# Two graph layers on one core: wider squares and a fifth difference buffer in the statistics pass, whole-megabyte loads and a shorter softmax tail in the score pass

## The chip, the cores and the metric

One core of a Trainium2 chip runs the whole program. The metric is the device time of one execution in microseconds (us); lower is better. Three runs of the kernel before are given, and one more execution was taken by the hardware profiler.

## The reference

The input x has 32 batches of 256 rows of 128 channels. A first graph attention layer and a layer norm give the x of the second layer, which is where the time goes and where the change lies. Cut to its core:

```python
D = jnp.abs(x[:, :, None, :] - x[:, None, :, :])          # every pair of rows of a batch
h = jnp.einsum('bijc,oc->bijo', D, W1) + b1                # 128 channels -> 64
m = jnp.mean(h, axis=(0, 1, 2)); v = jnp.mean((h - m) ** 2, axis=(0, 1, 2))
h = _leaky((h - m) / jnp.sqrt(v + EPS) * g1 + be1)
s = jnp.einsum('bijo,uo->biju', h, W2)[..., 0] + b2[0]
A = jax.nn.softmax(jnp.where(A_init > 0, s, NEG), axis=-1)
y = jnp.einsum('bij,bjc->bic', A, x)
y = y @ Wg.T + bg
y = _leaky((y - mean(y)) / sqrt(var(y) + EPS) * gg + beg)  # moments over batches and rows
out = jnp.concatenate([x, y], axis=2) @ Wt.T + bt          # then x + out, layer norm
```

The moments of h go over all pairs of all batches, so the pairs are passed over twice: once for the sums (the statistics pass), once for the scores (the score pass).

## The kernel before, in words

Channels lie on the 128 partitions. `ring` holds every batch transposed, each half followed by its own beginning, so that "row j minus row i" for many pairs is one subtraction of two windows of `ring`. By symmetry only half of the pairs are computed: 16 chunks of 2048 pairs for each batch. A chunk goes through TensorE with `w1t` (`project`, L872 to L877: four matmuls of 512 columns, two to each half of the partitions), and 128x1024 values of h come out in PSUM.

**Statistics pass.** The chunks of a batch are taken in the order `ORDER`. Five of them (`ON_PE`, positions 0, 3, 6, 9 and 12 of the order) get their differences from TensorE (`pick_differences`, L879) and their absolute value from ScalarE (L610, L612), the other eleven from VectorE: `subtract` (L1217) and then `absolute` (L1233, a bitwise AND), in groups of 2, 2, 2, 2 and 3 (`differences_between`). The differences stand in a ring of `ND` = 4 buffers `diff`: `subtract` of chunk c waits until chunk c - 4 has been projected. h goes to one of two PSUM buffers `hps`; TensorE may project chunk c (`stat_chunk`, L895) once ScalarE has read chunk c - 2. ScalarE's reader is `sum_h` (L614). Four chunks (`REDONE`: positions 0, 3, 6, 9) are squared straight from PSUM with a sum (L632) and thrown away. The other twelve are copied with a sum to one of eight buffers `tokeep` (L622), which SyncE stores to DRAM (`keep`, L386: `kept_one` holds the second halves of the four thrown-away ones' rectangles, 512 KB each, `kept_two` the rest), and after every second copy the two neighbouring copies are squared side by side, 2048 wide, with a sum (L627). The square waits on the copy just before it and writes to `spare`, a part of `yt` that nobody reads.

ScalarE's own order there is the program's: for each position j of a batch `sum_h(b, j)`, and behind it `absolute(b, j + 3)` where j + 3 is one of TensorE's.

**Score pass.** A batch is eight steps `kk`. At the even steps one thrown-away chunk is made again: VectorE's `differences` and `absolutes` (L1351, L1356, two buffers), TensorE's `again` (L936), and ScalarE's leaky activation out of PSUM into `fresh` (L654, 1024 wide). Beside it stands what was kept, loaded from DRAM by SyncE (`load_kept`, L404): at even steps one of four buffers `kept1` (1024 wide), at odd steps one of three buffers `kept2` (2048 wide). Each is activated in place (L654), and `score_products` (L943, four matmuls of 512 columns) adds the step to the batch's scores in PSUM. A load waits until the step that last used its buffer has been multiplied.

In between, spread over the next batches' steps, runs the softmax of the scores: `take_scores` (L670) copies them out, SyncE stores them (four DMAs) and reads them back as blocks (seven DMAs, L432), GpSimd masks (L511), VectorE adds masks (`add_upper` L1363, `masked` L1374), ScalarE takes exponentials (L682), TensorE transposes them (`transpose_probs`), ScalarE copies (L688), TensorE multiplies with x (`aggregate`), VectorE divides by the sum (`normalise_agg`, L1387), TensorE transposes back, ScalarE copies (`aggt_out`, L692), TensorE multiplies with Wg (`second_projection`), ScalarE adds bg and writes `yt` (`y_out`, L696), VectorE takes its moments and adds bt to the rows (`y_statistics`, L1396). The step at which each engine does each of these is written out by hand in a loop over `g` at the end of each engine's program, and every engine works strictly in that order. After the last batch the loops run on for 28 steps (`LAST`).

The last stage normalises y, multiplies with Wt, adds and normalises the rows and stores them.

## Time and profile before

| | us |
|---|---|
| median of 3 runs | 2411.68 (2410.97 to 2411.91) |
| the profiled execution | 2408.98, of which the trace spans 2406.7 |
| first layer, layer norm, ring | 0 to 373 of the span |
| statistics pass | 373 to 1678 |
| score pass | 1678 to 2358 |
| last stage | 2358 to 2407 |
| busy over the span | TensorE 84%, VectorE 88%, ScalarE 91% |
| granted TensorE clock, mean | 0.980 |

The stage bounds are the starts of the first `subtract` (372.7), of the first `differences` (1678.0) and of the last `y_statistics` (2358.0). The busy shares are means over stages that differ; what a stage costs is read below as a period, the time from one batch to the next, since both passes repeat exactly from batch to batch.

### The profile page before, as it was taken

The page shows a single profiled execution, that of the slowest core. Times are in us where ns is not written, and L with a number is a line of the kernel's source. Part 1 is how long each engine was busy: PE and PEld are TensorE (multiplying, and loading weights), DVE is VectorE, ACT ScalarE, POOL GpSimd, SP SyncE. Part 2 cuts the span into 40 slices and gives each one's busy share as a digit, 9 for nine tenths or more (in the row PEclk, how much of TensorE's full clock was granted, in tenths as well). Part 3 has the DMA queues.
Part 4 walks back from the last instruction along what each step waited for, and adds up shares of the span by engine and source line. Part 5 has one row for each costly group of instructions (what it writes and reads, how often), then busy time and mean ns, then how long its engine had stood idle before and what let it go on. Part 6 is the DMA issues. An engine that isn't in the chain of part 4 may idle for free.

```text
span 2406.7 us, 35438 instructions
## 1 busy us (share of the span) xinstructions
PE 2015.1 (84%) x12869; PEld 798.3 (33%) x12869; DVE 2112.7 (88%) x2615; ACT 2196.0 (91%) x3084; POOL 47.8 (2%) x50
## 2 busy tenths in 40 slices
PE   5777767888888888888888888887898988888986
PEld 4555543323232323232323232322122222222225
DVE  5888868999999999999999999998888888888866
ACT  5999977999999999999999999996999999999985
POOL 0000000000000000000000000000000001000000
PEclk8999989999999999999999999998999999999997
DMA  4111105444444444444444444444899899999962
GB/s 117 41 40 43 45 15 173 180 169 179 169 179 169 180 168 180 169 180 168 180 169 180 169 180 169 180 168 160 335 352 348 330 346 341 339 337 333 336 238 71
DMA packets 230499, 470.46 MB, mean 195 GB/s; under 512 B 53496, under 2 KB 144312, under 8 KB 213944
## 3 DMA queue, kind: packets, MB, share of 16 engines
q1 hardware_dynamic: 229264, 467.84, 52.4%
q8 instruction: 104, 1.70, 0.3%
q14 instruction: 67, 0.55, 0.1%
q10 hardware_dynamic: 1064, 0.36, 0.1%
HBM read 254.19 MB, written 213.91 MB: 194 GB/s over the span
## 4 chain that ended last, share of the span: by engine, by line
ACT 37%; DVE 26%; issue 19%; PE 17%; DMA 1%; ACTq 0%; SPq 0%; POOLq 0%; POOL 0%; DVEq 0%
PE banks L875 8%; ACT diff L610 7%; DVE diff L1222 6%; ACT hcopy L622 5%; ACT yt L627 5%; ACT habs L622 5%; DVE diff L1351 5%; ACT hcopy L654 4%; DVE ring L1094 4%; ACT habs L654 3%; PE banks L789 2%; ACT diff L654 2%; DVE diff L1236 2%; PE banks L799 2%; DVE ring L1112 1%
## 5 line engine op out<-in xcount | busy, mean ns | idle before, releaser
L875 PE MATMUL banks<-diff,w1t 128*64 128x512 f32 x5136 | 1211.7, 602 | 170.7 <-DVE diff L1236 56.3
L1222 DVE TENSOR_TENSOR diff<-ring 128x2048 f32<-128x2048 f32 x352 | 802.6, 2288 | 93.2 <-PE banks L875 93.2
L875 PEld LDWEIGHTS banks<-diff,w1t 128*64 128x64 f32 x5136 | 340.8, 136 | 906.6 <-issue 786.7
L1236 DVE TENSOR_SCALAR diff<-diff 128x2048 int32<-128x2048 int32 x354 | 415.5, 1220 | 0.0
L1351 DVE TENSOR_TENSOR diff<-ring 128x2048 f32<-128x2048 f32 x128 | 300.1, 2344 | 8.2 <-PE banks L875 8.0
L610 ACT ACTIVATE diff<-banks 128x2048 f32<-128x2048 f32 x128 | 238.4, 1862 | 1.8 <-PE banks L890 1.8
L622 ACT ACTIVATE hcopy<-banks 128x1024 f32<-128x1024 f32 x192 | 194.1, 1019 | 26.5 <-PE banks L875 26.5
L622 ACT ACTIVATE habs<-banks 128x1024 f32<-128x1024 f32 x192 | 194.0, 1019 | 25.9 <-PE banks L875 25.9
L627 ACT ACTIVATE yt<-hcopy,par 128x2048 f32<-128x2048 f32 x96 | 192.4, 2005 | 3.1
L627 ACT ACTIVATE yt<-habs,par 128x2048 f32<-128x2048 f32 x96 | 192.4, 2004 | 3.1
L890 PE MATMUL banks<-pick,yt 32*128 32x256 f32 x2560 | 183.8, 401 | 1.0 <-ACT ring L593 1.0
L654 ACT ACTIVATE diff<-diff,par 128x2048 f32<-128x2048 f32 x86 | 180.6, 2100 | 1.4 <-DMA diff<-kept_two 1.4
L958 PE MATMUL banks<-habs,w2s 128*32 128x512 f32 x768 | 134.9, 601 | 39.9 <-ACT hcopy L654 32.1
L654 ACT ACTIVATE hcopy<-hcopy,par 128x1024 f32<-128x1024 f32 (+1 forms) x106 | 166.4, 1579 | 0.1
L1356 DVE TENSOR_SCALAR diff<-diff 128x2048 int32<-128x2048 int32 x128 | 162.4, 1269 | 4.4
L654 ACT ACTIVATE habs<-banks,par 128x1024 f32<-128x1024 f32 x128 | 153.7, 1201 | 8.8 <-PE banks L875 8.8
L890 PEld LDWEIGHTS banks<-pick,yt 32*128 32x128 f32 x2560 | 115.7, 184 | 134.2 <-issue 129.4
L632 ACT ACTIVATE banks<-banks,par 128x1024 f32<-128x1024 f32 x128 | 136.4, 1066 | 7.6 <-PE banks L875 7.6
L541 ACT ACTIVATE ring<-ring,diff 128x256 f32<-128x256 f32 x256 | 129.0, 504 | 0.0
L542 ACT ACTIVATE ring<-ring,diff 128x256 f32<-128x256 f32 x256 | 128.9, 504 | 0.0
L1094 DVE CUSTOM_DVE_ANT_0 ring<-banks,adjt 128x256 f32<-128x256 f32 x256 | 90.8, 421 | 38.1 <-PE banks L789 38.1
L958 PE MATMUL banks<-hcopy,w2s 128*32 128x512 f32 x592 | 112.1, 605 | 0.0
(217 smaller groups left out, 1932.2 us busy)
## 6 DMA issues: line engine op xcount, KB each, us to landing
diff<-kept_two SPq DMA_DIRECT2D x86, 1024.0 KB, 7.2
kept_two<-hcopy SPq DMA_DIRECT2D x128, 512.0 KB, 2.9
kept_two<-habs SPq DMA_DIRECT2D x128, 512.0 KB, 2.9
hcopy<-kept_two SPq DMA_DIRECT2D x42, 1024.0 KB, 7.2
kept_one<-hcopy SPq DMA_DIRECT2D x64, 512.0 KB, 2.6
kept_one<-habs SPq DMA_DIRECT2D x64, 512.0 KB, 2.6
hcopy<-kept_one SPq DMA_DIRECT2D x64, 512.0 KB, 7.8
habs<-kept_one SPq DMA_DIRECT2D x64, 512.0 KB, 7.9
```

Of the source, the lines that this page charges most:

```text
L610: nc.scalar.activation(dst, dps, ACT.Abs, accum_out=column(EVENS + b * NR + REDONE.index(ORDER[j]))).then_inc(abs_pe, 1)
L622: nc.scalar.activation(tokeep[n % KB], h, ACT.Identity, accum_out=column(ODDS + n)).then_inc(kept_copied, 1)
L627: nc.scalar.activation(spare, src, ACT.Square, bias=par[:, 53:54], accum_out=column(SQUARES + B * NR + n // 2)).then_inc(sq_kept, 1)
L654: return nc.scalar.activation(dst, src, ACT.Prelu, scale=par[:, 38:39], bias=par[:, 39:40], alpha=0.01)
L875: last = nc.tensor.matmul(dst[half * O:(half + 1) * O, bank * BANK:(bank + 1) * BANK], w1t[:, :], src[:, m * BANK:(m + 1) * BANK], start=T ...
L890: last = nc.tensor.matmul(dst, xblk[b % 2][32 * m:32 * m + 32, e + s, :], pick[32 * m:32 * m + 32, :].rearrange("p (j i) -> p j i", j=BLK) ...
L958: last = nc.tensor.matmul(srp[b % 2][32 * t:32 * t + 32, :], w2s[:, WIN - top:WIN - top + 32], src, start=(kk == 0), stop=(kk == PAIRS - 1 ...
L1094: last = v.tensor_tensor_reduce(out=em[q][:, c:c + N], in0=ejp[:, h, :], in1=mneg[:, t * N:(t + 1) * N], scale=1.0, scalar=LOWEST, op0=ALU ...
L1222: v.tensor_tensor(shaped(diff[:, c % ND, :]), xj, xi_, ALU.subtract).then_inc(sub_done, 1)
L1236: v.tensor_scalar(bits, bits, ABS_BITS, None, ALU.bitwise_and).then_inc(abs_dve, 1)
L1351: v.tensor_tensor(shaped(diff[:, n % 2, :]), xj, xi_, ALU.subtract).then_inc(b_sub, 1)
L1356: v.tensor_scalar(bits, bits, ABS_BITS, None, ALU.bitwise_and).then_inc(b_abs, 1)
```

## The change

In the statistics pass `ND` becomes 5, a fifth difference buffer, which relaxes every wait on `ND` by one chunk. The kept copies are squared after every fourth copy instead of every second, four side by side, 4096 wide; the sums move to a later place of `yt`. Space for this comes from `band` (one mask instead of three) and from `aggt`.

In the score pass everything kept is one tensor of six units of 1 MB for each batch: two kept rectangles' second halves lie side by side in a unit that serves two even steps, and the odd steps have one unit each. So a batch has six loads and six activations of 2048, where it had four of each width. The units turn through five buffers; the buffer of unit m waits on the last step that used unit m - 5 (`UNIT_END`).

The softmax tail is shortened. x is multiplied with Wg and given bg first (`project_rows`, `take_rows`), the probabilities are divided by their sum before they are transposed (`scale_probs`), and the transposed probabilities then give y directly and transposed (`weigh_rows`). `aggregate`, `normalise_agg`, `transpose_agg`, `aggt_out` and `second_projection` go. The steps of the hand-written order move, and `LAST` is five steps shorter.

```diff
-    ND = 4
+    ND = 5
...
-    NS, NQ = 4, 3
+    UNIT_AT = (0, 1, 0, 2, 3, 4, 3, 5)
+    UNIT_STEP = (0, 1, 3, 4, 5, 7)
+    UNIT_END = (2, 1, 3, 6, 5, 7)
+    UNITS, NU = 6, 5
 
     EVENS, ODDS, SQUARES = 0, B * NR, B * NR + B * NK
-    SUMS = 5632
+    SUMS = 6912
     WIN = PAIRS + RECTS - 1
-    LAST = B * PAIRS + 28
+    LAST = B * PAIRS + 23
...
-        kept1 = [hcopy[:, 2, :], hcopy[:, 3, :], habs[:, 0, :], habs[:, 1, :]]
-        kept2 = [diff[:, 2, :], diff[:, 3, :], hcopy[:, 0:2, :].rearrange("p q n -> p (q n)")]
+        units = [hcopy[:, 0:2, :].rearrange("p q n -> p (q n)"), hcopy[:, 2:4, :].rearrange("p q n -> p (q n)"),
+                 habs[:, 0:2, :].rearrange("p q n -> p (q n)"), diff[:, 2, :], diff[:, 3, :]]
         fresh = [habs[:, 2, :], habs[:, 3, :]]
-        spare = yt[:, 4 * NP * C:4 * NP * C + CH]
+        spare = yt[:, 4 * NP * C:4 * NP * C + 2 * CH]
...
-                k, g = STEPS[kk], b * PAIRS + kk
-                if k < RECTS:
-                    n = b * RECTS + kk // 2
-                    if n >= NS:
-                        sp.wait_ge(sr_ready, g - 2 * NS + 1)
-                    sp.dma_start(kept1[n % NS], kept_one[b, k, :, :]).then_inc(one_loaded[n % NS], 16)
-                else:
-                    n = b * RECTS + kk // 2
-                    if n >= NQ:
-                        sp.wait_ge(sr_ready, g - 2 * NQ + 1)
-                    sp.dma_start(kept2[n % NQ], kept_two[b, k - RECTS, :, :]).then_inc(two_loaded[n % NQ], 16)
+                if kk not in UNIT_STEP:
+                    return
+                u = UNIT_STEP.index(kk)
+                m = b * UNITS + u
+                if m >= NU:
+                    sp.wait_ge(sr_ready, (m - NU) // UNITS * PAIRS + UNIT_END[(m - NU) % UNITS] + 1)
+                sp.dma_start(units[m % NU], kept[b, u, :, :]).then_inc(unit_loaded[m % NU], 16)
...
-                    if n % 2:
+                    if n % 4 == 3:
                         both = hcopy if n % KB < 4 else habs
-                        src = both[:, n % 4 - 1:n % 4 + 1, :].rearrange("p q n -> p (q n)")
+                        src = both[:, :, :].rearrange("p q n -> p (q n)")
                         act.wait_ge(kept_copied, n + 1)
                         nc.scalar.activation(spare, src, ACT.Square, bias=par[:, 53:54],
-                                             accum_out=column(SQUARES + B * NR + n // 2)).then_inc(sq_kept, 1)
+                                             accum_out=column(SQUARES + B * NR + n // 4)).then_inc(sq_kept, 1)
...
-                    act.wait_ge(one_loaded[n % NS], 16 * (n // NS + 1))
-                    leaky(kept1[n % NS], kept1[n % NS]).then_inc(b_act, 1)
-                else:
-                    act.wait_ge(two_loaded[n % NQ], 16 * (n // NQ + 1))
-                    leaky(kept2[n % NQ], kept2[n % NQ]).then_inc(b_act, 1)
+                if kk in UNIT_STEP:
+                    m = b * UNITS + UNIT_AT[kk]
+                    act.wait_ge(unit_loaded[m % NU], 16 * (m // NU + 1))
+                    leaky(units[m % NU], units[m % NU]).then_inc(b_act, 1)
...
-            def aggt_out(b):
-                act.wait_ge(aggt_ready, b + 1)
-                nc.scalar.activation(aggt[:, :], agp, ACT.Copy).then_inc(aggt_copied, 1)
-
             def y_out(b):
                 act.wait_ge(y_ready, b + 1)
-                nc.scalar.activation(bass.AP(yt, b * N, [[B * N, P], [1, N]]), yp, ACT.Identity,
-                                     bias=par[:, 5:6]).then_inc(y_copied, 1)
+                nc.scalar.activation(bass.AP(yt, b * N, [[B * N, P], [1, N]]), yp, ACT.Copy).then_inc(y_copied, 1)
...
-                if kk == 7 and 3 <= b <= B + 2:
-                    aggt_out(b - 3)
-                if kk == 2 and 4 <= b <= B + 3:
-                    y_out(b - 4)
+                if kk == 5 and 3 <= b <= B + 2:
+                    y_out(b - 3)
...
+            def project_rows(b):
+
+                if b >= 2:
+                    pe.wait_ge(y_copied, b - 1)
+                for t in range(NT):
+                    off = b * RING + t * WRAP
+                    last = nc.tensor.matmul(xgp[:, t * C:(t + 1) * C], ring[:, off:off + P], wgt[:, :], start=True, stop=True)
+                last.then_inc(xg_ready, 1)
...
-                pe.wait_ge(prob_ready, b + 1)
+                pe.wait_ge(prob_scaled, b + 1)
...
-            def aggregate(b):
+            def weigh_rows(b):
                 pe.wait_ge(probt_copied, b + 1)
-                if b:
-                    pe.wait_ge(y_copied, b)
-                for t in range(NT):
-                    for jt in range(NT):
-                        last = nc.tensor.matmul(agp[:, t * C:(t + 1) * C], probt[:, jt, t * P:(t + 1) * P],
-                                                bass.AP(rows, (NT * b + jt) * C, [[TILES * C, P], [1, C]]),
-                                                start=(jt == 0), stop=(jt == NT - 1))
-                last.then_inc(agg_ready, 1)
-
-            def transpose_agg(b):
-                pe.wait_ge(agg_copied, b + 1)
-                for t in range(NT):
-                    last = nc.tensor.transpose(agp[:, t * P:(t + 1) * P], agg[:, t, :], ident[:, :])
-                last.then_inc(aggt_ready, 1)
-
-            def second_projection(b):
-                pe.wait_ge(aggt_copied, b + 1)
-                nc.tensor.matmul(yp, wgt[:, :], aggt[:, :], start=True, stop=True).then_inc(y_ready, 1)
+                pe.wait_ge(xg_added, min(b + 2, B))
+                for jt in range(NT):
+                    last = nc.tensor.matmul(yp, bass.AP(yt, b * N + jt * C, [[B * N, P], [1, C]]), probt[:, jt, :],
+                                            start=(jt == 0), stop=(jt == NT - 1))
+                last.then_inc(y_ready, 1)
...
-                if kk == 0 and 3 <= b <= B + 2:
+                if kk == 1 and 3 <= b <= B + 2:
                     transpose_probs(b - 3)
                 if kk == 3 and 3 <= b <= B + 2:
-                    aggregate(b - 3)
-                if kk == 5 and 3 <= b <= B + 2:
-                    transpose_agg(b - 3)
-                if kk == 0 and 4 <= b <= B + 3:
-                    second_projection(b - 4)
+                    weigh_rows(b - 3)
+                if kk == 0 and 2 <= b <= B + 1:
+                    project_rows(b - 2)
...
-            def normalise_agg(b):
+            def scale_probs(b):
                 dve.wait_ge(prob_ready, b + 1)
                 v.reciprocal(small[:, 6:8], small[:, 4:6]).then_inc(den_ready, 1)
-                dve.wait_ge(agg_ready, b + 1)
                 dve.wait_ge(den_ready, b + 1)
                 for t in range(NT):
-                    last = v.tensor_scalar(agg[:, t, :], agp[:, t * C:(t + 1) * C], small[:, 6 + t:7 + t], None, ALU.mult)
-                last.then_inc(agg_copied, 1)
+                    last = v.tensor_scalar(prob[:, t, :], prob[:, t, :], small[:, 6 + t:7 + t], None, ALU.mult)
+                last.then_inc(prob_scaled, 1)
+
+            def take_rows(b):
+                dve.wait_ge(xg_ready, b + 1)
+                v.tensor_tensor(bass.AP(yt, b * N, [[B * N, P], [C, NT], [1, C]]), xgp.rearrange("p (t c) -> p t c", t=NT),
+                                bass.AP(bgb, 0, [[C, P], [0, NT], [1, C]]), ALU.add).then_inc(xg_added, 1)
...
+                if kk == 4 and 2 <= b <= B + 1:
+                    add_upper(b - 2)
                 if kk == 5 and 2 <= b <= B + 1:
-                    add_upper(b - 2)
-                if kk == 6 and 2 <= b <= B + 1:
                     masked(b - 2)
-                if kk == 5 and 3 <= b <= B + 2:
-                    normalise_agg(b - 3)
-                if kk == 3 and 4 <= b <= B + 3:
-                    y_statistics(b - 4)
+                if kk == 0 and 3 <= b <= B + 2:
+                    scale_probs(b - 3)
+                if kk == 6 and 3 <= b <= B + 2:
+                    y_statistics(b - 3)
+                if kk == 1 and 2 <= b <= B + 1:
+                    take_rows(b - 2)
```

Where the instructions stand now. ScalarE, in the statistics pass, from position 10 of a batch into the next batch, before (L622 the copy, L627 the square of two, L632 the square from PSUM, L610 and L612 the absolute values for TensorE's chunks):

```order
L612 ACTIVATE diff<-banks 128x2048
L622 ACTIVATE hcopy,yt<-banks 128x1024 x2
L627 ACTIVATE yt<-hcopy,par 128x2048
L622 ACTIVATE habs,yt<-banks 128x1024 x2
L627 ACTIVATE yt<-habs,par 128x2048
L610 ACTIVATE diff,yt<-banks 128x2048
L622 ACTIVATE habs,yt<-banks 128x1024 x2
L627 ACTIVATE yt<-habs,par 128x2048
L632 ACTIVATE banks,yt<-banks,par 128x1024
L610 ACTIVATE diff,yt<-banks 128x2048
L622 ACTIVATE hcopy,yt<-banks 128x1024 x2
L627 ACTIVATE yt<-hcopy,par 128x2048
```

and of the change (L626 the copy, L631 the square, L636 the square from PSUM, L614 and L616 the absolute values):

```order
L616 ACTIVATE diff<-banks 128x2048
L626 ACTIVATE habs,yt<-banks 128x1024 x2
L631 ACTIVATE yt<-habs,par 128x4096
L626 ACTIVATE hcopy,yt<-banks 128x1024 x2
L614 ACTIVATE diff,yt<-banks 128x2048
L626 ACTIVATE hcopy,yt<-banks 128x1024 x2
L631 ACTIVATE yt<-hcopy,par 128x4096
L636 ACTIVATE banks,yt<-banks,par 128x1024
L614 ACTIVATE diff,yt<-banks 128x2048
L626 ACTIVATE habs,yt<-banks 128x1024 x2
L636 ACTIVATE banks,yt<-banks,par 128x1024
L614 ACTIVATE diff,yt<-banks 128x2048
```

The square of two that stood behind every pair of copies is gone behind the first pair of each four, so that this pair is followed at once by the next chunk's work (L636 at position 3, L614 and more copies behind position 13), and the one square behind the fourth copy is 4096 wide.

VectorE, in the score pass, the second half of a batch's steps, before (L1351 and L1356 the differences and their absolute value, L1368 and L1372 `add_upper`, L1389 and L1393 `normalise_agg`, L1361 the mask, L1379 to L1385 `masked`):

```order
L1351 TENSOR_TENSOR diff<-ring 128x2048
L1356 TENSOR_SCALAR diff<-diff 128x2048
L1368 SCALAR_TENSOR_TENSOR adjt<-ub,par,adjt 128x512
L1372 TENSOR_TENSOR adjt<-adjt,diag 128x2x128
L1389 RECIPROCAL small<-small 128x2
L1393 TENSOR_SCALAR agg<-banks,small 128x128 x2
L1351 TENSOR_TENSOR diff<-ring 128x2048
L1356 TENSOR_SCALAR diff<-diff 128x2048
L1361 TENSOR_SCALAR adjt<-adjt 128x512
L1379 TENSOR_TENSOR adjt<-banks,adjt 128x384
L1381 TENSOR_REDUCE small<-adjt 128x2
L1385 TENSOR_SCALAR small<-small 128x2
```

and of the change, from the batch's first steps on (L1385 `scale_probs`, L1390 `take_rows`, L1344 and L1349 the differences and their absolute value, L1361 and L1365 `add_upper`, L1372 to L1378 `masked`):

```order
L1385 TENSOR_SCALAR prob<-prob,small 128x256 x2
L1390 TENSOR_TENSOR yt<-banks,bgb 128x256
L1344 TENSOR_TENSOR diff<-ring 128x2048
L1349 TENSOR_SCALAR diff<-diff 128x2048
L1344 TENSOR_TENSOR diff<-ring 128x2048
L1349 TENSOR_SCALAR diff<-diff 128x2048
L1361 SCALAR_TENSOR_TENSOR adjt<-ub,par,adjt 128x512
L1365 TENSOR_TENSOR adjt<-adjt,diag 128x2x128
L1372 TENSOR_TENSOR adjt<-banks,adjt 128x384
L1374 TENSOR_REDUCE small<-adjt 128x2
L1378 TENSOR_SCALAR small<-small 128x2
L1344 TENSOR_TENSOR diff<-ring 128x2048
```

The maxima that ScalarE's exponentials wait for (the last row of the first piece, the last but one of the second) are now made ahead of the batch's last differences instead of after them, the division stands with the batch's first steps and is 256 wide, and one addition over 256 columns (L1390) is new. `y_statistics` moves from step 3 to step 6.

## Rows read from the trace of the kernel before

**Rows 1.** Windows of one batch of each pass: from:to, length, busy by engine, clock, DMA.

```profile
1016.89:1056.98 40.09, 34.91 (x212) 12.25 (x213) 37.24 (x23) 38.28 (x53) 0.00 (x0) 1.00 0.45 174
1963.97:1984.46 20.49, 18.44 (x119) 5.47 (x115) 18.41 (x20) 19.52 (x20) 0.73 (x1) 1.00 0.91 340
```

**Rows 2.** Timeline of ScalarE, statistics pass: start, length, engine, line, what, [idle before].

```profile
1021.89 1.01 ACT L622 ACTIVATE habs<-banks 128x1024 f32<-128x1024 f32 x1
...
1022.88 1.02 ACT L622 ACTIVATE habs<-banks 128x1024 f32<-128x1024 f32 x1
...
1024.02 2.00 ACT L627 ACTIVATE yt<-habs,par 128x2048 f32<-128x2048 f32 x1
...
1026.02 1.07 ACT L632 ACTIVATE banks<-banks,par 128x1024 f32<-128x1024 f32 x1
...
1027.11 1.86 ACT L610 ACTIVATE diff<-banks 128x2048 f32<-128x2048 f32 x1
...
1028.96 1.02 ACT L622 ACTIVATE hcopy<-banks 128x1024 f32<-128x1024 f32 x1
...
1056.98 1.02 ACT L622 ACTIVATE hcopy<-banks 128x1024 f32<-128x1024 f32 x1 [1.62 <-PE banks L875]
```

**Rows 3.** Timeline of TensorE, the same batch (x8 is one chunk's four matmuls).

```profile
1023.13 1.94 PE L875 MATMUL banks<-diff,w1t 128*64 128x512 f32 x8 [1.63 <-ACT habs L622]
1025.00 1.15 PE L890 MATMUL banks<-pick,yt 32*128 32x256 f32 x16
1026.07 3.65 PE L875 MATMUL banks<-diff,w1t 128*64 128x512 f32 x16
...
1055.00 1.94 PE L875 MATMUL banks<-diff,w1t 128*64 128x512 f32 x8 [1.69 <-DVE diff L1236]
```

**Rows 4.** Timeline of VectorE, the end of the same batch.

```profile
1049.31 4.50 DVE L1222 TENSOR_TENSOR diff<-ring 128x2048 f32<-128x2048 f32 x2 [0.32 <-PE banks L875]
```

**Rows 5.** Groups by line and shape: busy us, mean ns, idle before.

```profile
L610 ACT ACTIVATE diff<-banks 128x2048 f32<-128x2048 f32 x128 | 238.4, 1862 | 1.8 <-PE banks L890 1.8
...
L654 ACT ACTIVATE diff<-diff,par 128x2048 f32<-128x2048 f32 x86 | 180.6, 2100 | 1.4 <-DMA diff<-kept_two 1.4
...
L632 ACT ACTIVATE banks<-banks,par 128x1024 f32<-128x1024 f32 x128 | 136.4, 1066 | 7.6 <-PE banks L875 7.6
...
L654 ACT ACTIVATE habs<-habs,par 128x1024 f32<-128x1024 f32 x64 | 80.2, 1252 | 0.0
```

**Rows 6.** Timeline of ScalarE, score pass.

```profile
1963.97 0.51 ACT L682 ACTIVATE prob<-adjt,small 128x256 f32<-128x256 f32 x1 [0.96 <-DVE small L1385]
...
1972.62 0.48 ACT L696 ACTIVATE yt<-banks,par 128x256 f32<-128x256 f32 x1
...
1984.47 0.51 ACT L682 ACTIVATE prob<-adjt,small 128x256 f32<-128x256 f32 x1 [0.98 <-DVE small L1385]
```

**Rows 7.** Timeline of VectorE, score pass.

```profile
1973.13 0.43 DVE L1398 BATCH_NORM_STATS2 row_stat<-yt 128x6 f32<-128x256 f32 x1 [1.73 <-ACT yt L696]
```

**Rows 8.** Groups by line and shape: the nearest to VectorE's new work.

```profile
L1393 DVE TENSOR_SCALAR agg<-banks,small 128x128 f32<-128x128 f32 x64 | 19.5, 347 | 4.8 <-PE banks L986 1.6
...
L1207 DVE TENSOR_SCALAR rows<-rows,mu,rstd 128x128 f32<-128x128 f32 x64 | 16.5, 340 | 0.0
...
L1104 DVE TENSOR_TENSOR diff<-banks,diff 128x256 f32<-128x256 f32 x32 | 13.6, 424 | 1.1
```

**Rows 9.** DMA issues on the page: count, KB each, median us to landing.

```profile
diff<-kept_two SPq DMA_DIRECT2D x86, 1024.0 KB, 7.2
...
hcopy<-kept_one SPq DMA_DIRECT2D x64, 512.0 KB, 7.8
```

**Rows 10.** Windows: a stretch of loads back to back, one without, and after the last activation.

```profile
1967.50:1982.50 15.00, 13.60 (x89) 4.08 (x93) 13.03 (x13) 15.00 (x14) 0.49 (x1) 1.00 1.00 403
1962.50:1966.00 3.50, 3.50 (x26) 0.88 (x19) 3.43 (x5) 2.54 (x7) 0.00 (x0) 1.00 0.44 113
2331.97:2357.97 26.00, 16.94 (x68) 11.30 (x69) 9.45 (x26) 8.64 (x26) 1.45 (x2) 0.64 0.10 23
```

More of the change, by code:

```diff
@@ L98, in gnn_pair_kernel @@
         adjt = sb("adjt", [P, 2, NT * N], I32)
-        band = sb("band", [P, 3, P])
+        band = sb("band", [P, P])
         ub = sb("ub", [P, 2, 4, P])
@@ L104, in gnn_pair_kernel @@
         btb = sb("btb", [P, C])
+        bgb = sb("bgb", [P, C])
         small = sb("small", [P, 64])
@@ L222, in gnn_pair_kernel @@
         kept_stored = [sem(f"kept_stored_{q}") for q in range(KB)]
-        one_loaded = [sem(f"one_loaded_{q}") for q in range(NS)]
-        two_loaded = [sem(f"two_loaded_{q}") for q in range(NQ)]
+        unit_loaded = [sem(f"unit_loaded_{q}") for q in range(NU)]
         pick_built = sem("pick_built")
@@ L309, in kept_before, with unit_of @@
             return sum(c not in REDONE for c in ORDER[:j])
+        def unit_of(k, tp):
+            step = STEPS.index(k)
+            return UNIT_AT[step], (k % 2 if k < RECTS else tp)
         def pe_before(j):
@@ L350, in _ @@
             sp.dma_start(par[:, 4:5], b2.rearrange("(a n) -> a n", a=1).to_broadcast([P, 1])).then_inc(par_loaded, 16)
-            for col, v in ((5, bg), (6, gg), (7, beg)):
+            for col, v in ((6, gg), (7, beg)):
                 sp.dma_start(par[:, col:col + 1], v.rearrange("(n a) -> n a", a=1)).then_inc(par_loaded, 16)
@@ L952, in score_products @@
                 for t in range(4):
-                    tp, cols = t // 2, slice((t % 2) * BANK, (t % 2 + 1) * BANK)
-                    if k < RECTS:
-                        src = kept1[n % NS][:, cols] if tp else fresh[n % 2][:, cols]
-                    else:
-                        src = kept2[n % NQ][:, tp * HC + (t % 2) * BANK:tp * HC + (t % 2 + 1) * BANK]
+                    tp, bank = t // 2, t % 2
+                    if k < RECTS and tp == 0:
+                        src = fresh[n % 2][:, bank * BANK:(bank + 1) * BANK]
+                    else:
+                        half = k % 2 if k < RECTS else tp
+                        src = units[m % NU][:, half * HC + bank * BANK:half * HC + (bank + 1) * BANK]
                     last = nc.tensor.matmul(srp[b % 2][32 * t:32 * t + 32, :], w2s[:, WIN - top:WIN - top + 32], src,
```

46 lines of the change are left out of this document (24 added, 22 removed).

## The prediction

> **What bounds the kernel now.** I began with windows over the stages and then took one batch of each pass, since both repeat. The statistics pass has a period of 40.09 us: ScalarE is busy 38.28, VectorE 37.24, TensorE 34.91 [rows 1]. ScalarE's timeline there runs without a gap but for one of 1.62 us a batch, in which it waits for TensorE [rows 2], which has itself stood 1.69 us for VectorE's absolute value [rows 3]; VectorE is late because its differences wait for a free buffer, 0.32 us before the last group, for instance [rows 4]. So ScalarE sets the pace, and the four buffers cost it 1.6 us. The score pass has a period of 20.49 us: ScalarE busy 19.52, VectorE 18.41, TensorE 18.44 [rows 1]. Its bound is a loop over two engines: VectorE waits 1.73 us for the `yt` of step 2 [rows 7], then works through to the maxima, and ScalarE's exponentials wait 0.98 us for those [rows 6]. From 1973.13 to 1984.47 the loop is on VectorE, from there to the next `yt` on ScalarE.
>
> **Statistics pass.** The sum of ScalarE's work falls. A square of two takes 2.00 us of the queue [rows 2]. No row has one of four. From 1024 to 2048 columns the time grows by 0.80 us (L632 to L610, out of PSUM) or 0.85 (L654, from SBUF to SBUF as here) [rows 5]; 2048 more columns give 3.59 or 3.70, against 4.00 for two squares apart, the dearest case. I take 3.70. With the wait on the copy before it, 1.14 from the copy's start to the square's where the next copy would start after 0.99 [rows 2], three fewer squares are worth 3 x (0.30 + 0.15) = 1.4 us a batch, and the fifth buffer could give the other 1.6: ScalarE alone would need 37.1, VectorE about as much.
>
> But the squares do a second job: each gives TensorE time to refill the two PSUM buffers. I follow ScalarE's new order with the intervals of the rows. A copy's start frees its buffer for TensorE 1.24 us later (1021.89 to 1023.13); chunk to `pick` 1.87, `pick` to chunk 1.07, chunk to next chunk 3.65 - 1.94 = 1.71; a chunk's start is 1.98 before ScalarE can read it (1055.00 to 1056.98); L632 takes 1.09 and L610 1.85 [rows 2, 3]. A batch starts with the reader of position 0 at 0, the absolute value at 1.09, copy 1 at 2.94, copy 2 at 3.93. Then no square follows, and position 3 is next, due at 4.92. Its chunk could start only when copy 1 had freed the buffer, at 4.18, and is ready at 6.16: 1.24 us of waiting. TensorE goes on with `pick` at 6.05, chunk 4 at 7.12, chunk 5 at 8.83, so copy 5 starts at 10.81 and the wide square at 11.95; it ends at 15.65. ScalarE's own work in this stretch is 13.7 us, so 1.9 are waits. Positions 6 to 11 are the same pattern, 15.65 again. In the last third copy 12 starts at 0, chunk 14 at 1.24, chunk 15 at 2.95, its copy at 4.93, the wide square at 6.07 and its end at 9.77. The period is 15.65 + 15.65 + 9.77 = 41.07 us, 0.98 more than the 40.09 measured, over 32 batches **+31 us**. VectorE, with five buffers, is ahead of every chunk in this chain, so the fifth buffer buys nothing here: its cover is the wait for ScalarE. With 3.59 for a square the pass is +21, with 4.00 it is +60.
>
> **Score pass, ScalarE.** Four activations of 1252 ns and four of 2100 become six of 2100 [rows 5]: 0.8 us a batch less. `aggt_out` goes (0.3 to 0.4 by the 256 columns of L696's 0.48 [rows 6]). ScalarE's work falls from 19.52 to about 18.5 [rows 1]. The loop above is cut: the maxima are made ahead of the last differences and the division and `y_statistics` stand where ScalarE has passed long before.
>
> **Score pass, VectorE.** It is next in line. Its queue needs 20.49 - 1.73 = 18.76 us a batch, the small waits on its own results included [rows 1, 7]. The two divisions grow from 128 to 256 columns: L1393 takes 347 ns and L1207, the same operation in SBUF, 340 [rows 8]; L1104's 424 for 256 columns bounds it above. I take 0.4 each, +0.12 a batch, between 0 and +0.15. `take_rows` is L1104's form, 0.42, in a queue some 0.34. Sum 19.2. TensorE does less than its 18.44 (four matmuls of 256 and 128 columns for seven). So the period becomes 19.2: 1.25 us x 29 batches = 36. The first three batches have no softmax beside them and only save ScalarE's 0.5, 1.5 in all. The drain after the last activation is 26.0 us [rows 10]; one engine hop in five goes, I take 2 and keep 0 and 6 for the range. Together **-40 us**.
>
> **Loads.** 340 GB/s over 20.49 us are 6.97 MB; back to back the queue moves 403 GB/s, and beside it stands a stretch of 3.5 us at 113 [rows 1, 10]. 17.3 us of transfer fit in 19.2. Merging loads saves nothing by itself: 512 KB land after 7.8 us, 1024 KB after 7.2 [rows 9], so place in the queue counts, not the number. The Trainium skill (DMA: Bandwidth & Descriptors, Anatomy of one DMA) gives every transfer a fixed 2.0 us and 436 GB/s beyond it, and would have us merge. An estimate from these figures, if the fixed part held the queue: eight transfers some 30 us a batch, six 26, a gain of over 100 us. The trace disagrees: eight fit in 20.49, the fixed part overlaps.
>
> The changed constants, `band` and the bias load are set-up work beside the first layer and cost nothing; if that cover went, a few tenths.
>
> **Sum.** +31 - 40 = -9, and I round the gain down to 8, since a schedule rarely closes as tightly as its bound. The profiled execution was 2409.0, so 2401 against it; the median of the runs is 2.7 higher, so **2404 us**, -0.3%. A measurement of this kernel tells about 0.2%, 4.8 us, from no change.
>
> **Rivals.**
> *The loads come late, slower.* The units of step 3 wait for the product of step 6, since a merged unit is held for three steps (`UNIT_END` 6), and are needed at step 3 of the next batch, some 3.7 steps of 2.4 = 8.9 us later; three megabytes are asked for within a microsecond or two. A landing of 7.2 [rows 9] fits; behind two others, 3 x 2.6 us of transfer at 403 GB/s and 2 of latency, the last takes 10, but that one is due later. It decides where landings pass 8.9 us. Then ScalarE stands before its in-place activations and the period stays near 20.5: 2411.7 + 31 - 2 = 2441. Half of that is as likely. For it: three engines within 4% of the new period leave no slack to catch up. Chance 0.15.
> *The ping-pong of ScalarE and TensorE costs less than I add up.* If ScalarE never waited, the pass would take 37.1 us a batch, 96 us less: 2411.7 - 96 - 40 = 2276. Halfway 2340. Against it: the 1.24 and 1.98 us are read off this very loop. Chance 0.07.
> *The clock.* It is 1.00 in both passes and 0.64 in the drain, where TensorE waits most of the time [rows 1, 10]. With longer stands the pass could fall to the lower level; sixteen chunks of 1.71 us would double and add 27 us a batch, some 880 in all: about 3290. My chain has TensorE standing at most 1.8 us, and 1.69 has been stood at 1.00 [rows 3]. The Trainium skill (TensorE: Matmul & The Clock Gate, Part 1) says that an idle TensorE is put back to 1.2 GHz; by that rule wider squares are a risk. Chance 0.01.
>
> **How the numbers follow.** My case has 0.77: in it faster 0.46, same 0.22, slower 0.09, since squares at 4.00 alone cost 29 us more. With the late loads (slower 0.12, same 0.03) and the cheap ping-pong (faster 0.07) and the clock (slower 0.01): faster 0.53, same 0.25, slower 0.22. The range goes from 2376 (squares at 3.59 -10, nothing added to VectorE -14, drain -4) to 2433 (squares at 4.00, or most of the late loads); outside lie the upper part of the late loads and the second rival, under 0.2.
>
> **What would show it.** Statistics period near 41.1 with no VectorE stall at all; ScalarE idle about 1.2 us before L636 of position 3 and 9; a square at 3.70. Score period 19.2, VectorE without waits, no activation waiting for a DMA. A statistics period below 40 would prove me wrong there, a score period above 20 in the other pass.

## The result, and the profile after

| | before | after |
|---|---|---|
| median, us | 2411.36 (8 runs, 2408.91 to 2412.13) | 2418.36 (8 runs, 2416.98 to 2421.75) |
| ratio | | 1.0035 [1.0025, 1.0044] |
| profiled execution, us | 2408.98 | 2421.01 |
| its span, us | 2406.7 | 2419.0 |
| mean granted clock | 0.980 | 0.979 |

The change makes the kernel 7.0 us slower; 2404 was forecast, 2376 to 2433 was the range. The profiled execution of the changed kernel, 2421.01, is among its slowest, so the two spans differ by 12.3 us where the medians differ by 7.0. Cut where the passes begin and end, they differ like this:

| stage | before | after | difference | forecast |
|---|---|---|---|---|
| up to the statistics pass | 372.7 | 374.0 | +1.3 | 0 |
| statistics pass | 1305.3 | 1337.3 | +32.0 | +31 |
| score pass with its drain | 680.0 | 657.8 | -22.2 | -40 |
| last stage | 48.7 | 49.9 | +1.2 | 0 |

One pass came out as worked out. The other gave a little over half of its gain, and that turns the sign. The +1.3 and +1.2 are no cost of the change: in the other kernels with the same set-up the statistics pass starts between 372.1 and 373.9, and their last stages take 48.5 to 50.1. The two windows of one batch each in the changed kernel, statistics pass and score pass, columns as in [rows 1]:

```profile
1044.20:1085.36 41.16, 34.99 (x210) 12.51 (x208) 37.26 (x23) 37.64 (x49) 0.00 (x0) 1.00 0.44 170
1963.00:1982.80 19.80, 18.44 (x119) 5.38 (x112) 19.38 (x22) 19.14 (x19) 1.08 (x1) 1.00 0.94 360
```

Against [rows 1], the statistics batch takes 41.16 for 40.09 us although ScalarE is busy 0.64 us less: it waits more. The score batch takes 19.80 for 20.49. Over batches 1 to 28 of each pass the means of the periods are 40.09 and 41.16, and 20.5 and 19.79.

**Statistics pass.** ScalarE's timeline of the changed kernel, around the kept copies 0 to 3 of one batch, beside [rows 2]:

```profile
1062.83 1.02 ACT L626 ACTIVATE habs<-banks 128x1024 f32<-128x1024 f32 x1
...
1063.83 1.02 ACT L626 ACTIVATE habs<-banks 128x1024 f32<-128x1024 f32 x1
...
1066.06 1.09 ACT L636 ACTIVATE banks<-banks,par 128x1024 f32<-128x1024 f32 x1 [1.11 <-PE banks L871]
...
1070.73 1.03 ACT L626 ACTIVATE habs<-banks 128x1024 f32<-128x1024 f32 x1 [0.60 <-PE banks L871]
...
1071.87 3.71 ACT L631 ACTIVATE yt<-habs,par 128x4096 f32<-128x4096 f32 x1
```

TensorE's timeline of the same microseconds, beside [rows 3]:

```profile
1061.22 1.94 PE L871 MATMUL banks<-diff,w1t 128*64 128x512 f32 x8 [1.57 <-ACT banks L636]
1064.08 1.94 PE L871 MATMUL banks<-diff,w1t 128*64 128x512 f32 x8 [0.93 <-ACT habs L626]
```

The copy that starts at 1062.83 frees its buffer for the chunk at 1064.08, 1.25 us later. The chunk is read at 1066.06, 1.98 after its start. ScalarE, with no square to do meanwhile, stands 1.11 us, and 0.60 us again before the next copy. So the two engines hand one pair of buffers back and forth, and each waits for the other. Summed over 1200 us of the pass, the waits of ScalarE, then those of TensorE, in the changed kernel (line <- what it waited for: us in total, times, longest):

```profile
ACT banks L636 <- PE banks L871: 64.7, 58, 1.1
ACT habs L626 <- PE banks L871: 17.9, 30, 0.6
ACT hcopy L626 <- PE banks L871: 16.7, 28, 0.6
```

```profile
PE banks L871 <- ACT banks L636: 79.9, 59, 1.6
PE banks L871 <- ACT hcopy L626: 49.6, 59, 1.3
PE banks L871 <- ACT habs L626: 49.0, 58, 1.3
```

1200 us are 29.2 batches, so ScalarE stands twice a batch at each place, 99.3 / 29.2 = 3.4 us in all. TensorE never waits for VectorE here.

From the page of the changed kernel, beside [rows 5], first the two kinds of squares of the statistics pass, then two of the in-place activations of the score pass:

```profile
L636 ACT ACTIVATE banks<-banks,par 128x1024 f32<-128x1024 f32 x128 | 137.9, 1078 | 79.3 <-PE banks L871 79.3
...
L631 ACT ACTIVATE yt<-hcopy,par 128x4096 f32<-128x4096 f32 x48 | 178.1, 3710 | 1.6
...
L658 ACT ACTIVATE diff<-diff,par 128x2048 f32<-128x2048 f32 x76 | 158.1, 2092 | 15.4 <-DMA diff<-kept 15.2
L658 ACT ACTIVATE hcopy<-hcopy,par 128x2048 f32<-128x2048 f32 x78 | 162.2, 2093 | 10.7 <-DMA hcopy<-kept 10.5
```

**Score pass.** With the same wait in the group on `habs`, 6.4, ScalarE stands 32.1 us before its in-place activations until a load has landed, in 43 places; in [rows 5] that was 1.4. Loads take longer to land than in [rows 9], by the page's DMA issues:

```profile
hcopy<-kept SPq DMA_DIRECT2D x78, 1024.0 KB, 8.3
```

Why one of them comes late stands in SyncE's timeline of a batch (start, time spent on issuing, line, what):

```profile
2035.87 0.33 SPq L419 DMA_DIRECT2D hcopy<-kept  x1
2036.24 1.82 SPq L432 DMA_DIRECT2D ring_scores<-sring  x4
2038.10 0.42 SPq L419 DMA_DIRECT2D habs<-kept  x1
2040.08 0.34 SPq L419 DMA_DIRECT2D diff<-kept  x1
2044.38 0.58 SPq L445 DMA_DIRECT2D ub<-ring_scores  x1
2045.01 0.61 SPq L447 DMA_DIRECT2D ub<-ring_scores  x1
2045.66 0.61 SPq L449 DMA_DIRECT2D ub<-ring_scores  x1
2046.31 2.56 SPq L453 DMA_DIRECT2D ub<-ring_scores  x4
2048.91 1.77 SPq L419 DMA_DIRECT2D diff<-kept  x1
```

At step 7 SyncE issues a load of a megabyte and behind it the four small stores of the scores (L432). At step 2 it wants to read those scores back as blocks (L445) and must have them landed. It stands from 2040.42 to 2044.38, issues seven block loads for 4.5 us, and only then the load of step 3. Averaged over batches 6 to 26 of the pass, that load is issued 5.1 us before ScalarE wants its data, where I had reckoned 8.9, and lands 5.3 after its issue: no slack is left. Of the 32.1 us of waits, 13.7 stand before the activation of step 3 (17 places) and 11.6 before that of step 5 (14 places), whose load leaves 1.1 to 2.3 us behind the one of step 3 and so is held up with it. What SyncE waited for over the score pass:

```profile
SPq L419 <- PE banks L956: 128.7, 70, 4.8
SPq L445 <- DMA ring_scores<-sring: 121.8, 30, 5.4
```

The second row is 4.1 us a batch of a queue that stands for its own stores. In the kernel before, SyncE stands for them too, 1.7 us a batch, without any activation waiting for it:

```profile
SPq L442 <- DMA ring_scores<-sring: 46.6, 27, 4.0
```

Two theories followed. For the statistics pass: the wide squares alone cost time, and the fifth buffer helps, or does nothing. For the score pass: the small stores queue behind the megabytes and hold up the load of step 3; the rival says that VectorE is simply 0.6 us dearer than the forecast.

### The profile page after: what moved, and what is told of

Read it like the earlier page. It is cut to its first block, busy times and chain, and to the rows that moved or that the text cites. A ratio compares the mean times of both kernels' runs of the same rounds, so it can differ in the third digit from the quotient of the medians.

```text
span 2419.0 us, 34833 instructions
## 1 busy us (share of the span) xinstructions
PE 2001.6 (83%) x12741; PEld 802.6 (33%) x12741; DVE 2127.0 (88%) x2647; ACT 2148.5 (89%) x2796; POOL 42.4 (2%) x50
## 3 DMA queue, kind: packets, MB, share of 16 engines
q8 instruction: 103, 1.69, 0.3%
## 4 chain that ended last, share of the span: by engine, by line
PE 31%; ACT 29%; issue 16%; DVE 12%; DMA 9%; SPq 3%; ACTq 0%; POOLq 0%; POOL 0%; DVEq 0%
PE banks L871 18%; ACT diff L614 7%; ACT hcopy L626 5%; ACT habs L626 4%; DVE ring L1086 4%; DMA ring_scores<-sring 3%; DVE diff L1214 3%; ACT yt L631 3%; PE banks L886 3%; ACT habs L658 3%; DMA diff<-kept 3%; PE banks L956 3%; PE banks L785 2%; ACT banks L636 2%; DMA hcopy<-kept 2%
## 5 line engine op out<-in xcount | busy, mean ns | idle before, releaser
L1214 DVE TENSOR_TENSOR diff<-ring 128x2048 f32<-128x2048 f32 x352 | 797.7, 2289 | 125.0 <-PE banks L871 121.6
L871 PEld LDWEIGHTS banks<-diff,w1t 128*64 128x64 f32 x5136 | 349.2, 137 | 937.9 <-issue 813.0
L1228 DVE TENSOR_SCALAR diff<-diff 128x2048 int32<-128x2048 int32 x354 | 415.6, 1221 | 0.0
L1344 DVE TENSOR_TENSOR diff<-ring 128x2048 f32<-128x2048 f32 x128 | 292.6, 2286 | 17.4 <-PE banks L871 17.3
L614 ACT ACTIVATE diff<-banks 128x2048 f32<-128x2048 f32 x128 | 239.4, 1870 | 1.3 <-PE banks L886 1.3
L626 ACT ACTIVATE habs<-banks 128x1024 f32<-128x1024 f32 x192 | 195.1, 1020 | 20.8 <-PE banks L871 20.8
L626 ACT ACTIVATE hcopy<-banks 128x1024 f32<-128x1024 f32 x192 | 195.1, 1020 | 19.7 <-PE banks L871 19.7
L636 ACT ACTIVATE banks<-banks,par 128x1024 f32<-128x1024 f32 x128 | 137.9, 1078 | 79.3 <-PE banks L871 79.3
L956 PE MATMUL banks<-habs,w2s 128*32 128x512 f32 x816 | 159.6, 602 | 55.5 <-ACT hcopy L658 24.6
L631 ACT ACTIVATE yt<-hcopy,par 128x4096 f32<-128x4096 f32 x48 | 178.1, 3710 | 1.6
L631 ACT ACTIVATE yt<-habs,par 128x4096 f32<-128x4096 f32 x48 | 178.1, 3710 | 1.6
L1349 DVE TENSOR_SCALAR diff<-diff 128x2048 int32<-128x2048 int32 x128 | 169.0, 1320 | 4.4
L658 ACT ACTIVATE diff<-diff,par 128x2048 f32<-128x2048 f32 x76 | 158.1, 2092 | 15.4 <-DMA diff<-kept 15.2
L658 ACT ACTIVATE hcopy<-hcopy,par 128x2048 f32<-128x2048 f32 x78 | 162.2, 2093 | 10.7 <-DMA hcopy<-kept 10.5
L658 ACT ACTIVATE habs<-banks,par 128x1024 f32<-128x1024 f32 x128 | 153.0, 1196 | 8.8 <-PE banks L871 8.8
```

What stands on the lines that cost most here:

```text
L614: nc.scalar.activation(dst, dps, ACT.Abs, accum_out=column(EVENS + b * NR + REDONE.index(ORDER[j]))).then_inc(abs_pe, 1)
L626: nc.scalar.activation(tokeep[n % KB], h, ACT.Identity, accum_out=column(ODDS + n)).then_inc(kept_copied, 1)
L631: nc.scalar.activation(spare, src, ACT.Square, bias=par[:, 53:54], accum_out=column(SQUARES + B * NR + n // 4)).then_inc(sq_kept, 1)
L636: nc.scalar.activation(h, h, ACT.Square, bias=par[:, 53:54], accum_out=column(SQUARES + b * NR + REDONE.index(ORDER[j]))).then_inc(sq_redo ...
L658: return nc.scalar.activation(dst, src, ACT.Prelu, scale=par[:, 38:39], bias=par[:, 39:40], alpha=0.01)
L871: last = nc.tensor.matmul(dst[half * O:(half + 1) * O, bank * BANK:(bank + 1) * BANK], w1t[:, :], src[:, m * BANK:(m + 1) * BANK], start=T ...
```

## The experiments

Each is the changed kernel with one edit, unless it says otherwise. A ratio is against the kernel before, timed beside it; its median there was 2409.99 to 2411.03, against 2411.36 beside the changed kernel, so a difference from the 2418.36 of the changed kernel can be off by some 1.4 us.

**Squares of two, five buffers.** A table says behind which kept copy a square stands and how many copies it takes.

```diff
+    SQ_AT = {1: 2, 3: 2, 5: 2, 7: 2, 9: 2, 11: 2}
...
-                    if n % 4 == 3:
+                    if n % NK in SQ_AT:
+                        wide = SQ_AT[n % NK]
```

> The changed kernel with its squares back at two copies, 2048 wide, behind every second copy; five difference buffers and the new score pass stay. Theory (a square behind every pair of copies covers TensorE's refill of the two PSUM buffers): no ScalarE wait at L636 any more, statistics period 38.3 us instead of 41.16, total 2418.4 - 2.85 x 32 = about 2327 us. Rival (the fifth buffer gives nothing, the pass returns to what it was): period 40.1, total about 2384.

Measured: 2332.0, ratio 0.9675 [0.9659, 0.9691]. One batch of its statistics pass in a window:

```profile
1059.06:1097.44 38.38, 34.70 (x212) 12.42 (x208) 37.25 (x23) 38.19 (x55) 0.00 (x0) 1.00 0.47 181
```

The total is 5 us above the 2327 expected. The period is 38.38, of which ScalarE is busy 38.19, and over 1200 us it has not one wait. The wide squares cost 2418.36 - 2332.0 = 86.4 us. They do save ScalarE 0.55 us of work a batch (38.19 to 37.64), and lose 3.4 by taking away the cover of TensorE.

**Four buffers with the wide squares.**

```diff
-    ND = 5
+    ND = 4
```

> The changed kernel with four difference buffers instead of five, squares 4096 wide. Theory (in the chain of the wide squares VectorE needs the fifth buffer not to be late at the last group too): statistics period 41.9, total about 2443 us. Rival (as my prediction had it, VectorE is ahead of every chunk and the chain is ScalarE's and TensorE's alone, so the buffer gives nothing): period 41.2, total 2418.

Measured: 2480.02, ratio 1.0284 [1.0269, 1.03], 61.7 us above the changed kernel. TensorE's timeline (one batch, then the next), and then windows over these two batches and over 2 us behind the first stand:

```profile
1104.17 2.62 PE L871 MATMUL banks<-diff,w1t 128*64 128x512 f32 x8 [2.30 <-DVE diff L1228]
...
1147.80 1.94 PE L871 MATMUL banks<-diff,w1t 128*64 128x512 f32 x8 [2.30 <-DVE diff L1228]
```

```profile
1073.67:1117.30 43.63, 36.33 (x208) 12.83 (x208) 37.26 (x23) 37.91 (x49) 0.00 (x0) 0.96 0.42 160
1117.30:1159.30 42.00, 34.70 (x208) 12.33 (x208) 37.16 (x23) 37.89 (x50) 0.00 (x0) 1.00 0.43 166
1106.20:1108.20 2.00, 2.00 (x18) 1.22 (x16) 1.56 (x2) 1.11 (x2) 0.00 (x0) 0.50 0.61 250
```

With four buffers VectorE is late once a batch and TensorE stands 2.30 us for it. The batches without a slower clock, 12 of 31, take 42.00, as expected (41.9). The other 19 take some 43.6, since the clock goes to 0.50, the lower of its two levels, behind the stand. The mean is 42.96. That slower clock, some 1 us a batch, is most of what the total lies above the 2443 expected. The forecast's sentence that the fifth buffer buys nothing falls: it is worth 1.8 us a batch beside wide squares, of which 0.84 is the stand (42.00 to 41.16) and the rest goes with the clock.

**Squares of two, four buffers** (both edits above). This leaves only the new score pass.

> The changed kernel with squares of two and four difference buffers, so the statistics pass of the kernel before beside the new score pass. Theory: statistics period 40.1 (the fifth buffer is worth 1.7 us a batch only where squares of two cover TensorE), total 2332 + 1.72 x 32 = about 2387 us. It also prices the new score pass alone against the kernel before: 2411 - 24 = 2387. Rival (the fifth buffer is worth the same beside wide squares as beside narrow ones): the other runs gave 1.8 us between four and five buffers with wide squares, of which some is clock, so this one would come out at the same 2387 and only the stalls in its trace tell where they lie.

Measured: 2385.51, ratio 0.99 [0.9885, 0.9915]. The statistics period is 40.11, that of before. The fifth buffer is worth 1.73 us a batch beside squares of two (40.11 to 38.38), so the "only" of this expectation does not hold beside the 1.80 of the run above. The change has three parts, from 2410.11 (before, beside this run): score pass -24.6, fifth buffer 2332.0 - 2385.5 = -53.5, wide squares +86.4. They add to +8.3; +7.0 was measured. The last two depend on their order: beside wide squares the fifth buffer gave 61.7.

**One wide square a batch**, behind copies 0 to 3, where its missing partner uncovers TensorE; and then behind copies 8 to 11, in the batch's last third.

```diff
+    SQ_AT = {3: 4, 5: 2, 7: 2, 9: 2, 11: 2}
```

> As the run with squares of two and five buffers (38.38 us a batch, 2332 us), but the first four copies of each batch squared once, 4096 wide, behind position 5. Theory (what counts is the missing cover in front of position 3, where TensorE has a pick to do as well): the whole 1.5 us of that place come back, statistics period 39.9, total about 2380 us. Rival (a wide square costs the same wherever it stands, a third of the 2.78 us between 38.38 and 41.16): period 39.3, total 2361.

Measured: 2377.04, ratio 0.9865 [0.9849, 0.9882]; period 39.89. Its ScalarE timeline has the stand of the changed kernel, once a batch:

```profile
1068.49 1.09 ACT L639 ACTIVATE banks<-banks,par 128x1024 f32<-128x1024 f32 x1 [1.12 <-PE banks L874]
```

```diff
+    SQ_AT = {1: 2, 3: 2, 5: 2, 7: 2, 11: 4}
```

> As the run with squares of two and five buffers (38.38 us, 2332 us), but the last four copies of each batch (positions 12 to 15) squared once, 4096 wide. Theory (behind position 13 an absolute value of 1.85 us stands in the order and covers TensorE's refill in place of the square): almost free, period 38.6, total about 2338 us. Rival (the same cost wherever it stands): 39.3, 2361. Rival (a wider square saves its fixed part): 37.9, 2318.

Measured: 2338.69, ratio 0.9702 [0.9687, 0.9716]; period 38.57. Against 38.38 for squares of two, the first place costs 1.51 us, the last 0.19. Twice the first and once the last make 3.21, and all three together are 41.16 - 38.38 = 2.78, so the places are not quite independent. The price is in the place: a width of 4096 costs 1.51 us in one and 0.19 in the other.

**Stores ahead of the load**, on SyncE at step 7.

```diff
+                if kk == 7 and 1 <= b <= B:
+                    store_scores(b - 1)
                 if b < B:
                     load_kept(b, kk)
...
-                if kk == 7 and 1 <= b <= B:
-                    store_scores(b - 1)
```

> The changed kernel with one move on SyncE: at step 7 the four stores of the scores are issued ahead of the load of that step's unit, not behind it. Theory (the score pass waits for loads because the stores land behind megabytes in the queue, SyncE stands for them, then issues seven block loads, and only then the load of step 3): the stores land about 2.5 us earlier, the load of step 3 is issued up to 2.5 us earlier, the waits at L658 mostly go, score period 19.8 -> 19.3 us, total about 2403 us. Rival (the queue's bytes are the bound): period and total unchanged, 2418, waits at L658 as before.

Measured: 2394.4, ratio 0.9931 [0.9916, 0.9945], 24.0 us below the changed kernel, where 15 were expected; score period 18.95. SyncE's timeline and, under it, its waits over the pass:

```profile
2023.94 1.74 SPq L432 DMA_DIRECT2D ring_scores<-sring  x4
2027.36 0.34 SPq L419 DMA_DIRECT2D hcopy<-kept  x1
2027.74 0.44 SPq L419 DMA_DIRECT2D habs<-kept  x1
2031.56 0.32 SPq L419 DMA_DIRECT2D diff<-kept  x1
2031.99 0.58 SPq L445 DMA_DIRECT2D ub<-ring_scores  x1
```

```profile
SPq L419 <- PE banks L956: 167.6, 86, 3.4
SPq L432 <- ACT sring L677: 65.7, 30, 4.9
SPq L445 <- DMA ring_scores<-sring: 4.0, 4, 1.9
```

The blocks follow the last load at once; the wait for the stores falls from 121.8 to 4.0 us. The load of step 3 is issued 7.0 us ahead of its use and lands after 6.5. ScalarE's waits for loads are now 5.2 + 2.3 + 1.2 = 8.7 us, 23.4 less than before this edit, which is the gain; 13.0 of it come back before step 3 and 9.7 before step 5. That the stores now make SyncE wait 2.2 us a batch for `sring` shows in no wait of ScalarE or VectorE. Two hundred microseconds of this kernel:

```profile
2000.00:2200.00 200.00, 186.79 (x1171) 57.55 (x1171) 196.04 (x210) 196.51 (x178) 10.32 (x11) 1.00 0.99 363
```

VectorE is busy 98% (189.33 of 200 in the changed kernel) and waits for others 5 us in the whole pass: it is the bound that the forecast named. ScalarE and the DMA engines (0.99) are as full, so that VectorE alone sets the 18.95 is not shown.

**Block loads from GpSimd.** The seven go out from GpSimd's program, ahead of its mask.

```diff
             for b in range(B):
+                load_blocks(b)
                 mask_blocks(b)
```

> The changed kernel with the seven block loads of the scores issued by GpSimd instead of SyncE. Theory (SyncE's 4.4 us of issuing and its wait for the stores delay the load of step 3): that load is issued 3 to 5 us earlier, waits at L658 go, score period near 19.2 us, total about 2400 us. Rival 1 (bytes are the bound): unchanged at 2418. Rival 2 (GpSimd's issuing slows VectorE or lands the blocks late, so that TensorE waits at the transposes of the scores): period above 20, total above 2425.

Measured: 2403.18 (2398.81 to 2408.55), ratio 0.9971 [0.9958, 0.9983]; score period 19.27. This takes SyncE's stand away by another way: the stores land as late as ever, and GpSimd waits for them. ScalarE's waits for loads fall to 10.4 us. In six places it now waits for TensorE, 6.4 us in all, and in each of the six TensorE had itself just stood 1.5 to 2.2 us before the transposes of the scores, for GpSimd's mask. Over the pass this wait is:

```profile
PE banks L965 <- POOL ub L512: 30.1, 15, 3.3
```

So rival 2's mechanism is there in part, at a small price.

**Stores later**, behind the load of the next batch's step 0.

```diff
-                if kk == 7 and 1 <= b <= B:
-                    store_scores(b - 1)
+                if kk == 0 and 2 <= b <= B + 1:
+                    store_scores(b - 2)
```

> The changed kernel with the stores of the scores issued one load later instead of one earlier (behind the load of the next batch's first unit). Theory (the place of the stores in the queue sets when SyncE is free for the load of step 3): that load comes some 2 us later than in the changed kernel, score period 21 to 21.5 us instead of 19.8, total about 2455 us. Rival (the bytes are the bound, the place is not): unchanged, 2418.

Measured: 2493.66, ratio 1.0348 [1.0332, 1.0363], 75.3 us above the changed kernel, twice what I expected. ScalarE's waits for loads (from the trace's list on L658), and a window:

```profile
  DMA diff<-kept: 43.5, 23
  DMA hcopy<-kept: 42.7, 25
  DMA habs<-kept: 21.8, 13
```

```profile
1900.00:2000.00 100.00, 88.54 (x496) 24.70 (x496) 84.07 (x90) 85.29 (x79) 5.83 (x4) 0.90 0.81 312
```

The waits are 108.0 us, 75.9 more than in the changed kernel, which is the difference measured. 90.6 of them, in 30 places, stand before the activation of step 3, whose load is now issued only 2.2 us before its data are wanted. The clock averages 0.90 here; whether it lengthens these waits or only goes with them was not separated. The direction is as expected: the later the stores land, the later the loads behind the blocks.

**The same order in the kernel before**, as a control: the edit of the stores ahead of the load.

> The kernel before, with the stores of the scores issued ahead of step 7's load. Theory (before, no activation waits for a load, the loop of VectorE and ScalarE over yt and the maxima sets the period, so the place of the stores counts for nothing): score period 20.5, total unchanged at 2411 us. Rival (the earlier stores are a gain of their own in any order): about 20 us less, 2390.

Measured: 2410.84 against 2410.11, ratio 1.0001 [0.9991, 1.001]. There the loop of VectorE and ScalarE [rows 6, 7] sets the period, and between 1740 and 2300 us no activation waits for a load. The order of the stores is worth nothing before the change and 24 us after it.

**Both repairs**, squares of two and stores first, the rest as in the changed kernel.

> Both mends together: squares of two and the stores of the scores ahead of step 7's load. If the two places are independent, their gains add: 2418.4 - 86 - 24 = 2308 us, statistics period 38.4, score period 18.95. If the score pass's gain in the earlier run hung on something of the statistics pass, less.

Measured: 2306.63 (2304.25 to 2308.5), ratio 0.9569 [0.9555, 0.9583]. Windows over the score pass and the statistics pass:

```profile
1900.00:2100.00 200.00, 187.74 (x1176) 57.17 (x1172) 195.90 (x210) 196.25 (x180) 12.06 (x10) 1.00 0.99 366
1000.00:1100.00 100.00, 91.20 (x548) 32.61 (x546) 96.64 (x58) 99.51 (x139) 0.00 (x0) 1.00 0.46 177
```

This beats both kernels, by 103 us the one before. 86.4 and 24.0 us were the gains apart, 111.7 together: two passes that don't touch each other.

## Why the prediction was wrong

- **Statistics pass: right.** +32.0 for +31, period 41.16 for 41.07, square 3.71 for 3.70, ScalarE idle 1.11 for 1.24 at the places named. The chain over the two PSUM buffers was read off the loop itself, and the one-place experiments show the cost place by place. ScalarE's waits are 3.4 us a batch where the chain has 3.9.
- **"The fifth buffer buys nothing here": wrong, without weight in the sum.** VectorE is ahead of every chunk only because there are five. With four the pass takes 42.96 a batch. I had compared the chain with the kernel before, whose squares gave VectorE time, and not with four buffers beside wide squares. Squares of two would have shown the 1.7 us that the fifth buffer gives.
- **Score pass, the step that failed: the period.** "So the period becomes 19.2": it is 19.80, 0.6 x 29 = 17 us of the 18 missing. VectorE's work was not the error: with the loads on time the period is 18.95, below the 19.2, and the new score pass gives 24.6 + 24.0 = 48.6 us, more than the 40. So the waits for loads, a term that the sum has at nothing, cost 24.0 us, and a period taken some 0.25 too long hid a part of that. The division takes 350 ns for 400, `take_rows` 422 for 420. TensorE, said to do less than its 18.44, is busy 18.44 in the window above.
- **The step under it: "Loads. 17.3 us of transfer fit in 19.2."** The capacity is there, the share stands at 0.99 with stores first. But I counted megabytes and not the order of one queue: in these runs what is issued behind a megabyte lands behind it, and an engine that waits for such a landing holds up all that it would issue next. That is the overlap that the prediction had wrong: SyncE stands 4.1 us a batch, issues the load of step 3 only 5.1 us ahead, and ScalarE waits. I wrote "place in the queue counts" and did not follow SyncE through a batch; its 46.6 us of standing were there in the trace of the kernel before.
- **The late loads (0.15, 2441): half of it came true.** The mechanism, an activation that stands for a load of step 3, is what happened, though step 5 has nearly as much of the 32.1 us of waits (11.6 to 13.7). Its price was 37 us on the forecast, and 17 came, 24.0 by the run with the stores first. Its cause was put wrongly: not the product of step 6 frees the buffer too late; SyncE is not there to issue. What the Trainium skill gives (DMA: Bandwidth & Descriptors, Anatomy of one DMA), 2.0 us fixed for each, would by my estimate have made the merging worth over 100 us; the runs exclude that estimate, -24.6 for the whole new score pass. It is the estimate that they exclude: the section is on transfers that GpSimd issues, where these are SyncE's, and it does not say that the fixed part holds the queue.
- **The drain:** 26.0 [rows 10] became 23.7 us, from 2345.38 to 2369.10; 24 was forecast.
- **The ping-pong cheaper (0.07):** excluded; 3.4 us of waits a batch are there.
- **The clock (0.01):** 1.00 in both windows of the changed kernel, and TensorE's stands in its statistics pass reach 1.57. It was nearer than 0.01 says: with four buffers the stand is 2.30 us and the lower level comes, and in the score pass of the changed kernel it comes twice, behind stands of 2.03 and 2.00 us. The Trainium skill (TensorE: Matmul & The Clock Gate, Part 1) says that an idle TensorE is put back to 1.2 GHz; in the four-buffer run this followed 19 of 31 stands of 2.30 us and not the other 12.

The range held the time. The direction did not, since a gain of 8 us was the rest of two terms of 31 and 40, and one of them carried a queue that I had not walked through.

## What to carry to other kernels

Where two engines hand a pair of buffers to each other, the long instruction in between is their cover: merging it saves its fixed part and uncovers the refill, so ask of each merged instruction what stood in its place. When a change cuts a loop, walk every queue through one period in its order of issue, a DMA queue too, and look there for anything that waits for a landing. A small transfer whose landing is waited for goes ahead of the large ones, if anything stands behind that wait; in the kernel before nothing did, and the same move gave nothing.

## What the runs showed of the hardware

- **A stand of TensorE and its clock.** In the four-buffer kernel TensorE stands 2.30 us once in every batch, always in the same place. After 19 of 31 stands the clock is 0.50 for a few microseconds (the window from 1106.20), after the other 12 it stays at 1.00 (the batch from 1117.30). In the changed kernel's score pass it fell behind a stand of 2.03 us that ended at 2169.72, and behind one of 2.00 us that ended at 2258.82. Stands of 1.57 to 1.69 us, in the statistics passes of the kernels before and after, were never followed by it. What tells one stand of 2.30 us from the next is open.

```profile
2170.40:2173.90 3.50, 3.50 (x14) 1.41 (x12) 2.08 (x2) 3.31 (x4) 0.92 (x1) 0.51 0.89 363
```

- **Small stores behind large loads.** Four score stores, issued behind a load of a megabyte in the same queue from 2036.24 on, had landed at 2044.37, some 8 us later. Issued from 2023.94 on, ahead of it, they were no longer waited for at 2031.99. In each of the batches 6 to 26 of the changed kernel the last store landed 0.65 to 0.87 us after the load issued ahead of it, and before the next load; 8.2 us after the first store's issue on average, 6.6 with the stores first.
- **GpSimd beside VectorE.** An absolute value (L1349) takes 1.23 us, and about 1.63 nearly once a batch, while GpSimd masks its blocks. VectorE's and then GpSimd's timeline of the changed kernel:

```profile
2047.32 1.23 DVE L1349 TENSOR_SCALAR diff<-diff 128x2048 int32<-128x2048 int32 x1
...
2051.84 1.63 DVE L1349 TENSOR_SCALAR diff<-diff 128x2048 int32<-128x2048 int32 x1
```

```profile
2051.60 0.79 POOL L514 TENSOR_TENSOR ub<-ub,band 128x256 f32<-128x256 f32 x1 [18.22 <-DMA ub<-ring_scores]
```

GpSimd's span overlaps the longer of the two. Of the 128 in the pass, 28 take 1.6 us or more and the other 100 take 1.23, so this costs some 0.4 us a batch.
